# Sorting edges by destination before a graph layer: two buckets per scan, and sorted blocks added into DRAM tables by GpSimd

## The reference

```python
edge_index = jnp.stack([src, dst])                      # src is sorted differently from dst
# layer 0:  first row of edge_index is the target, second the source
w0f, w1f = x @ w0, x @ w1
x = layernorm(x + relu(w0f + segment_sum(w1f[edge_index[1]], edge_index[0], N)))
# layer 1: relational attention, 8 edge types, 8 heads of 32; softmax over each target's edges
x = layernorm(x + attention(x, W, attn_src, attn_dst, edge_index, edge_type))
```

## Time and profile before

| | us |
|---|---|
| median of 3 runs (2782.86 to 2790.21) | 2787.57 |
| span of the profiled execution | 2782.6 |
| DVE's first operation in the loop of moves | 134.99 |
| POOL's first gather of y | 288.67 |

### The profile page before, as it was taken

How to read it: one execution, slowest core, us unless ns; L and a number is a source line. 1 busy time by engine, 2 the same in 40 slices (tenths; PEclk the granted TensorE clock), 3 DMA queues, 4 the chain that set the end, 5 groups by cost and what they waited for, 6 DMA issues and landing times.

```text
span 2782.6 us, 38039 instructions
## 1 busy us (share of the span) xinstructions
PE 2296.5 (83%) x9879; PEld 1645.9 (59%) x9879; DVE 1984.8 (71%) x4237; ACT 1685.5 (61%) x3537; POOL 1843.1 (66%) x1874
## 2 busy tenths in 40 slices
PE   7866688899999999999988578777777777777775
PEld 4454566677777777777764456555555555555541
DVE  8999475555556555555553578888888888888887
ACT  4399455566666666566653466656656655665643
POOL 0000677777777777777771777777777777777745
PEclk9888799999999999999998688888888889888888
DMA  4300545764444444444454454545445545545535
GB/s 133 104 1 1 164 116 151 179 225 152 160 152 160 153 159 153 158 155 155 150 138 157 133 147 139 138 139 147 136 138 143 144 137 140 146 139 137 141 93 157
DMA packets 177746, 387.53 MB, mean 139 GB/s; under 512 B 42638, under 2 KB 106836, under 8 KB 171011
## 3 DMA queue, kind: packets, MB, share of 16 engines
q0 software_dynamic: 83888, 233.09, 30.6%
q1 hardware_dynamic: 86594, 99.05, 11.8%
q10 hardware_dynamic: 7056, 52.99, 4.9%
HBM read 302.96 MB, written 82.03 MB: 138 GB/s over the span
## 4 chain that ended last, share of the span: by engine, by line
PE 39%; POOL 24%; issue 12%; DVE 10%; DMA 9%; ACT 4%; DVEq 2%; SPq 0%; POOLq 0%; ACTq 0%; PEldq 0%
PE ps L1647 18%; POOL region L1287 15%; PE ps L1685 8%; POOL region L1245 7%; PE ps L1749 6%; DMA region<-ha_d,idx_t 5%; DVE nodes L839 4%; DMA region<-y_d,edge_z 3%; PE ps L1558 3%; ACT region L1374 2%; DVE nodes L721 1%; PE ps L1609 1%; PE ps L1732 1%; DVE region L444 1%; POOL region L1304 1%
## 5 line engine op out<-in xcount | busy, mean ns | idle before, releaser
L1245 POOL DMA_INDIRECT region<-y_d,edge_z x856 | 878.5, 1026 | 548.6 <-DVE edge_z L605 286.9
L1287 POOL DMA_INDIRECT region<-ha_d,idx_t x880 | 897.1, 1019 | 310.6 <-issue 240.8
L721 DVE TENSOR_TENSOR nodes<-ps,nodes 128x512 f32 x856 | 592.2, 692 | 491.4 <-PE ps L1647 377.7
L1647 PE MATMUL ps<-region 128*128 128x256 f32 x3424 | 794.3, 385 | 72.7 <-DMA region<-y_d,edge_z 26.3
L1647 PEld LDWEIGHTS ps<-region 128*128 128x128 f32 x3424 | 650.0, 192 | 249.2 <-issue 115.5
L1749 PE MATMUL ps<-region 128*128 128x264 f32 x1760 | 618.5, 482 | 163.5 <-DVE nodes L839 119.9
L1749 PEld LDWEIGHTS ps<-region 128*128 128x128 f32 x1760 | 347.5, 224 | 359.7 <-DVE nodes L839 237.1
L839 DVE TENSOR_TENSOR nodes<-ps,nodes 128x264 f32 x880 | 373.6, 425 | 52.1 <-DVE nodes L839 42.5
L1409 ACT ACTIVATE region<-iota_n,edge_z 128x256 f32<-128x256 f32 x856 | 364.7, 499 | 68.0 <-PE ps L1647 63.3
L1685 PE MATMUL ps<-region,edge_z 128*128 128x512 f32 x784 | 363.0, 592 | 3.3 <-ACT edge_z L1431 2.4
L1443 ACT COPY region<-ps 128x512 f32<-128x512 f32 x196 | 114.6, 587 | 350.7 <-PE ps L1685 289.6
(11 more groups left out here) (243 smaller groups left out, 1977.4 us busy)
## 6 DMA issues: line engine op xcount, KB each, us to landing
ha_d<-region ACTq DMA_DIRECT2D x49, 1056.0 KB, 4.7
region<-near_d SPq DMA_DIRECT2D x55, 512.0 KB, 5.0
region<-ha_d,idx_t POOLq DMA_INDIRECT x880, 3.3
region<-y_d,edge_z POOLq DMA_INDIRECT x856
edge_z<-level_d SPq DMA_DIRECT2D x55, 136.0 KB, 3.3
kl_d<-region SPq DMA_DIRECT2D x8, 903.0 KB, 15.5
edge_z<-kl_d SPq DMA_DIRECT2D x55, 129.0 KB
y_d<-edge_z SPq DMA_DIRECT2D x25, 256.0 KB, 3.2
```

The costliest lines, as they stand in the source:

```text
L721: v.tensor_tensor(into, ps[:, u, :], into, ALU.add).then_inc(added0, 1)
L1245: g.indirect_dma_start(rows0[c % RING][:, u, :], None, y_d, bass.IndirectOffsetOnAxis(ap=y_idx[:, k:k + 1], axis=0), bounds_check=node_bou ...
L1287: g.indirect_dma_start(rows[s][:, k, :], None, ha_rows, bass.IndirectOffsetOnAxis(ap=idx_t[:, B * b + k:B * b + k + 1], axis=0), bounds_ch ...
L1647: mm = t.matmul(ps[:, u, h * D:(h + 1) * D], lhsT=sel0[c % SEL][:, u, h * P:(h + 1) * P], rhs=rows0[c % RING][:, u, :], start=True, stop=True)
```

## The change

- Buckets are taken in pairs: 13 masks of the pair (9 on DVE, 4 on ACT) whose value is 1 for the even and 4096 for the odd bucket. So one count and one scan carry both; counts, starts and q are packed and unpacked by shifts and ands. The scans are 13.
- `wide` and its broadcast go. DVE and POOL make `jumps` over 104 windows x 25 buckets (2600 elements) between scans, DVE sums it to `goes_row`, and PE turns it behind y tile 20, for which PE waits.
- A window has 32 cells. A move still takes 28 columns of edges, but as two groups of 14, each with its own 104 windows in its own half of the bank; the matmuls are 28 of 104 by 64 columns. DVE sums high and low part into `stage` (four buffers).
- POOL adds each group's 104 rows of 32 cells into a table in DRAM by an indirect DMA that accumulates (60 in all). There are three tables in turn, and the n-th place waits until the (n-3)-th has landed. SP fills the tables with zeros early and reads them back at the end in two parts; DVE adds the three, PE turns them, ACT copies the cells out. `halves`, `S_c` and `settle` go.
- y tiles 36 to 49 are made in the loop, one behind each second move. In it ACT makes the Abs of its next window in four parts.

```diff
-    PP = 4
-    TB = PP * BLK
-    NBT = -(-(-(-E // KR)) // PP)
-    HC = P // 2
-    WW = (TB * P + BK * (2 * HC - 2)) // HC
+    PP = 2
+    TBG = PP * BLK
+    TB = 2 * TBG
+    NBT = -(-(-(-E // KR)) // (2 * PP))
+    NG2 = 2 * NBT
+    HC = P // 4
+    WW = (TBG * P + BK * (2 * HC - 2)) // HC
+    NPAIR = -(-BK // 2)
+    HIGH = 4096
+    NTAB = 3
     COLS = -(-((E + BK * (P - 1)) // P) // 8) * 8
     NG = COLS // 4
     RING = 5
     SEL = 3
-    OH = COLS // 2
-    MASKED = 18
-    EARLY = BK - MASKED
-    WIDE_AT, WAB_AT = 20, 28
+    OH = 4 * P
+    MASKED = 9
+    EARLY = 6
+    GOES_AT, WAB_AT, Q_AT = 20, 28, 35
+    WROWS = KR * P // HC
...
+    place_d = [dram(f"place{n}_d", [WROWS, HC], F32) for n in range(NTAB)]
...
+            do(v.tensor_scalar(bit_i, loc_i, 1, None, ALU.bitwise_and))
+            do(v.tensor_scalar(pair_i, src_i, 9, None, ALU.logical_shift_right))
+            do(v.tensor_scalar(shift_i, bit_i, 12.0, None, ALU.mult))
+            do(v.tensor_scalar(c_row, bit_i, float(HIGH - 1), 1.0, ALU.mult, ALU.add))
+            do(v.tensor_copy(pair, pair_i))
             for t in range(MASKED):
-                v.tensor_scalar(masks[t], bt, float(t), 0.0, ALU.is_equal, ALU.add,
-                                accum_out=cnt[:, t:t + 1]).then_inc(masked, 1)
+                v.scalar_tensor_tensor(out=masks[t], in0=pair, scalar=float(t), in1=c_row, op0=ALU.is_equal, op1=ALU.mult,
+                                       accum_out=cnt_all[:, t:t + 1]).then_inc(masked, 1)
+            v.wait_ge(masked, MASKED)
+            v.wait_ge(counted, NPAIR - MASKED)
+            do(v.tensor_copy(cnt_i[:, 0, :], cnt_all))
+            do(v.tensor_scalar(cnt_i[:, 1, :], cnt_i[:, 0, :], 12, None, ALU.logical_shift_right))
+            do(v.tensor_scalar(cnt_i[:, 0, :], cnt_i[:, 0, :], HIGH - 1, None, ALU.bitwise_and))
+            v.tensor_copy(cnt, cnt_i.rearrange("p b t -> p t b")).then_inc(counted, 1)
...
-            do(v.scalar_tensor_tensor(out=start, in0=base, scalar=float(-HC), in1=before_p, op0=ALU.mult, op1=ALU.add))
-            do(v.scalar_tensor_tensor(out=start, in0=start, scalar=-1.0, in1=col_128, op0=ALU.add, op1=ALU.add))
-            SU["wd"] = n[0]
-            v.wait_ge(masked, MASKED)
-            v.wait_ge(counted, BK - MASKED)
+            do(v.scalar_tensor_tensor(out=starts, in0=base, scalar=float(-HC), in1=before_p, op0=ALU.mult, op1=ALU.add))
+            do(v.tensor_tensor(starts, starts, col_128, ALU.add))
+            do(v.scalar_tensor_tensor(out=start_all, in0=start[:, :, 1], scalar=float(HIGH), in1=start[:, :, 0],
+                                      op0=ALU.mult, op1=ALU.add))
...
-            for t in range(BK):
+            for t in range(NPAIR):
                 if t == 1:
                     v.wait_ge(sort_in, IN["v"])
                 if t >= 2:
                     v.wait_ge(summed, t)
-                v.tensor_tensor_scan(ranks[t % 2], ones[:, 0:1].to_broadcast([P, KR]), masks[t], start[:, t:t + 1],
+                v.tensor_tensor_scan(ranks[t % 2], ones[:, 0:1].to_broadcast([P, KR]), masks[t], start_all[:, t:t + 1],
                                      ALU.mult, ALU.add).then_inc(scans, 1)
                 if t >= 1:
                     put(t - 1)
-            put(BK - 1)
-
-
-            v.wait_ge(sort_in, IN["wide"])
-            do(v.scalar_tensor_tensor(out=jumps, in0=wide[:, :, 0:BK], scalar=part[:, 0:1], in1=wide[:, :, BK:2 * BK],
-                                      op0=ALU.is_le, op1=ALU.mult))
-            do(v.tensor_reduce(goes_f, jumps, X, ALU.add))
-            do(v.tensor_scalar(goes_i, goes_f, part[:, 0:1], None, ALU.add))
-            do(v.tensor_scalar(col_i, goes_i, 1, None, ALU.logical_shift_right))
-            do(v.tensor_scalar(odd_i, goes_i, 1, None, ALU.bitwise_and))
-            do(v.tensor_copy(goes_col, col_i))
-            SU["goes"] = n[0]
-            do(v.tensor_copy(sides[:, 1, :], odd_i))
-            do(v.tensor_scalar(sides[:, 0, :], sides[:, 1, :], -1.0, 1.0, ALU.mult, ALU.add))
-            v.tensor_scalar(part_i, v_col, 11, 4, ALU.logical_shift_right, ALU.logical_shift_left).then_inc(split_made, 1)
-            v.tensor_scalar(v_col, v_col, 2047, None, ALU.bitwise_and).then_inc(split_made, 1)
-            v.wait_ge(split_made, 2)
-            v.tensor_copy(v_high, part_i).then_inc(split_made, 1)
-            v.tensor_scalar(v_low, v_col, 2.0 ** -7, None, ALU.mult).then_inc(split_made, 1)
+                if t == 1:
+                    v.tensor_tensor(jumps, iota_row[:, 0:WW].unsqueeze(2).to_broadcast([P, WW, BK]),
+                                    wd[:, 0, :].unsqueeze(1).to_broadcast([P, WW, BK]), ALU.is_ge).then_inc(goes_made, 1)
+                if t == NPAIR // 2:
+                    v.wait_ge(goes_made, 2)
+                    do(v.tensor_reduce(goes_row, jumps, X, ALU.add))
+                    v.tensor_tensor(goes_row, goes_row, iota_row[:, 0:WW], ALU.add).then_inc(goes_made, 1)
+                if t == NPAIR // 2 + 1:
+                    v.tensor_scalar(part_i, v_col, 11, 4, ALU.logical_shift_right, ALU.logical_shift_left).then_inc(split_made, 1)
+                    v.tensor_scalar(v_col, v_col, 2047, None, ALU.bitwise_and).then_inc(split_made, 1)
+                if t == NPAIR // 2 + 2:
+                    v.wait_ge(split_made, 2)
+                    v.tensor_copy(v_high, part_i).then_inc(split_made, 1)
+                    v.tensor_scalar(v_low, v_col, 2.0 ** -7, None, ALU.mult).then_inc(split_made, 1)
+            put(NPAIR - 1)
+            v.wait_ge(summed, NPAIR + 1)
+            do(v.tensor_copy(place_i, q_row))
+            do(v.tensor_tensor(place_i, place_i, shift_i, ALU.logical_shift_right))
+            do(v.tensor_scalar(place_i, place_i, HIGH - 1, None, ALU.bitwise_and))
+            v.tensor_copy(q_row, place_i).then_inc(summed, 1)
...
-            def halves_of(k):
+            def stage_of(k):
                 v.wait_ge(moved, k + 1)
-                if k >= 2:
-                    v.wait_ge(o_ps, k - 1)
-                v.tensor_tensor(halves[k % 2][0:WW, :, :, :],
-                                ps[0:WW, 2 + k % 2, 0:2 * HC].rearrange("p (v n) -> p v n", v=2).unsqueeze(2)
-                                .to_broadcast([WW, 2, 2, HC]),
-                                sides[0:WW, :, k].unsqueeze(1).unsqueeze(3).to_broadcast([WW, 2, 2, HC]),
-                                ALU.mult).then_inc(halves_made, 1)
+                if k >= 4:
+                    for n in range(2 * k - 8, 2 * k - 6):
+                        v.wait_ge(placed[n % NTAB], 16 * (n // NTAB + 1))
+                v.tensor_reduce(stage[k % 4][0:WW, :, :],
+                                ps[0:WW, 2 + k % 2, 0:4 * HC].rearrange("p (s v n) -> p s n v", s=2, v=2),
+                                X, ALU.add).then_inc(staged, 1)
...
+            sp.wait_ge(iotas, 3)
+            sp.wait_ge(w_in, 32)
+            for n in range(NTAB):
+                sp.dma_start(place_d[n].rearrange("(p w) e -> p (w e)", p=P), zeros).then_inc(w_in, 16)
...
+            for n in range(NTAB):
+                sp.wait_ge(placed[n], 16 * ((NG2 - n + NTAB - 1) // NTAB))
+            for h, (first, end) in enumerate(CELLS):
+                end = min(-(-end // P) * P, KR)
+                for n in range(NTAB):
+                    sp.dma_start(table[n][:, first:end].rearrange("c (b s) -> c b s", s=P),
+                                 place_d[n].rearrange("(b c w) e -> c b (w e)", c=P, w=P // HC)
+                                 [:, first // P:end // P, :]).then_inc(table_in[h], 16)
...
+            g.wait_ge(goes_made, 1)
+            g.tensor_tensor(jumps, jumps, wd[:, 1, :].unsqueeze(1).to_broadcast([P, WW, BK]), ALU.mult).then_inc(goes_made, 1)
+
+            def place(n):
+                if n == 0:
+                    g.wait_ge(sort_in, IN["goes"])
+                    g.wait_ge(w_in, 16 * (NTAB + 3))
+                if n % 2 == 0:
+                    g.wait_ge(staged, n // 2 + 1)
+                if n >= NTAB:
+                    g.wait_ge(placed[n % NTAB], 16 * (n // NTAB))
+                g.indirect_dma_start(place_d[n % NTAB], bass.IndirectOffsetOnAxis(ap=goes_i[0:WW, PP * n:PP * n + 1], axis=0),
+                                     stage[n // 2 % 4][0:WW, n % 2, :], None, bounds_check=place_bound, oob_is_err=True,
+                                     compute_op=ALU.add).then_inc(placed[n % NTAB], 16)
+
+            for n in range(NG2):
+                place(n)
...
+            windows_of(0, 0, TB)
             for k in range(NBT):
-                columns_of(k)
-                if k % 4 == 1 and k + 3 < NBT:
-                    windows_of(k + 3)
+                ahead = k // 4 * 4 + 4
+                if ahead < NBT:
+                    windows_of(ahead, TBG // 2 * (k % 4), TBG // 2 * (k % 4) + TBG // 2)
+                if y_tile_at(k) is not None:
+                    keep_products(y_tile_at(k))
...
```

(44 more changed lines are left out.)

184 lines of the change are left out of this document (97 added, 87 removed).

## The result

The changed kernel takes 2807.82 us (median of four runs, 2804.39 to 2812.3) against 2787.45 of the kernel before on the same chip: 1.0071 times as long, 95% interval 1.0055 to 1.0087. I had forecast 2740. The profiled execution after is the one of 2804.39 us, 1.8 more than its span. The span grew by 20.0 us. 18.0 of them lie ahead of the first gather of y, which starts at 306.70 and not at 288.67; behind it the work takes 2495.9 us, where it took 2493.9. So the question is the sort alone, 65.2 us from the forecast start (241.5) to the real one.

What follows compares the result with a forecast made beforehand. Before the loop PE's order was the bound; in it ACT and DVE were nearly full. First place at 126.4, 59 steps of 1.75 and a tail of 11.8 put the gather at 241.5, 47.2 sooner: 2787.6-47.2 = 2740.4 us, range 2722 to 2780.

Steps and rivals of the forecast that it cites:

- That is 1.72 a place: GpSimd's queue in the loop: each place takes 1.32 us of issue and gap plus 0.41 of hold.
- the queue is the bound by little: Loop of moves: GpSimd's queue at 1.75 us a place sets the pace, against 1.69 for the engines.
- Issue: GpSimd's queue: issuing one place costs 1.01 us, as a row gather does, and 0.30 until the next.
- Hold: GpSimd's queue: DVE operations with two SBUF inputs lengthen a place by 0.41 us on average.
- the landing: Loop: a place's round trip of 5.2 us, three in flight, allows one place per 1.75 us.
- the tail: From the last place's issue to the first gather of y: landing, loads, additions and shift take 11.8 us.
- The engines' own loop: Loop: a circle of move, Abs, kept tile and Relu takes 3.4 us a move; last move ends at 222.6.
- The gain ahead of the loop: Before the loop: fewer masks, scans and y tiles let PE turn q at 107, 22.5 us sooner.
- The first: Rival, loop: places hide wholly and the engines set the pace; gather at 236.4, -52.3 us, 2735; chance 0.26.
- The second: Rival, loop: a place's round trip is long, 6 to 7 us; -30 to -10 us, middle 2762; chance 0.20.
- third: Rival, loop: round trip from 7.5 us puts the gather behind 288.67; at 10 us +52, 2840; chance 0.10.
- DVE alone as the bound: Loop, variant of the rival with hidden places: DVE's 12.4 us for four moves set the pace; -58 us, 2729.

Runs made afterwards that it cites:

- e2: Changed kernel with the 60 places as plain indirect writes that replace rows, without the addition: 2772.58 us (one execution).
- e1: Changed kernel with DVE waiting in the loop for the end of each operation on two SBUF inputs before the next: 2760.56 us, 0.9913 of the kernel before.
- e4: Changed kernel with no places issued, only counted as landed, so y is gathered from row 0: 3189.94 us; moves 3.6 us each.
- e8: Changed kernel with both the DVE waits of e1 and the plain writes of e2: 3058.12 us, beside 3105.15 for the kernel before on that chip.
- e3: Changed kernel with two tables in DRAM instead of three: 2802.24 us (one execution).
- e7: Changed kernel with DVE's windows operation, from the fifth move, replaced by an equally long reduce with one SBUF input: 140.6 us from first to last place.
- e6: Changed kernel with one DVE wait a move, ahead of the windows: 0.9995 of the kernel before.

## Why the prediction was wrong

The step that failed is "That is 1.72 a place", and with it "the queue is the bound by little". The place was taken at 1.42 us of issue and hold, and took 2.46. Both terms were too small, and one for a reason that the rows could have given.

- Issue: I took 1.01 us from gathers, which add nothing. With the addition it is 1.60 (e2 against the changed kernel). 0.59 more a place, 35 us over 59 steps.
- Hold: I took +0.41 as a mean of three gathers beside fp32 operations. It was 2.46-1.60 = 0.86: 0.45 more, 27 us. The 0.41 was no property of the operations but of the gaps around them. Of the operations in the earlier trace rows the first ends at 488.50, and the others lie as far apart as in e1 (lines below). Each held gather there ends 0.89 behind the end of the one operation that it began under: 489.39 against 488.50, 492.83 against 491.94. In the loop up to four operations follow without a gap, 3.3 us in all, and the longest hold was 2.99 (4.59-1.60).

```profile
488.53 1.09 DVE L676 TENSOR_TENSOR region<-region 128x896 f32<-128x896 f32 x1
...
490.85 1.09 DVE L679 TENSOR_TENSOR region<-region 128x896 f32<-128x896 f32 x1
```

35 and 27 make the 62 us by which the first-to-last time of the places (165.2) passes its forecast (103.2); the 0.34 us between two places, for 0.30, is what I had added for the landing (1.75 for 1.72). The rest of the 65.2 is small: the first place 1.75 later (128.15, not 126.4), the tail 13.4 and not 11.8. The engines' own loop, 3.6 us a move and not 3.4 (e4), hides under the queue. The 27 us are the hold beyond what I had allowed for. The whole hold is 0.86 a place, 51 us, and e1 brings it down to 0.15 with nothing but gaps: 0.71 less a place, 42 us, which is what the places and the first gather gained (42.2 and 42.4). The division above is one of busy times, not of what each term would bring alone: without the addition (e2) the places gained 29.7 us, not 34.

What held: counts at 24.7 (26.1), scans from 39.4 (40.6), `goes_row` at 69.7 (68.0), q_row at 94.95 (93.7), q turned at 108.4 (107); in brackets the forecasts. The gain ahead of the loop is there: 21.1 us at the first move. The loop with its tail took 182.5 us from there (306.70-124.19), where it took 143.4: 39.1 were lost.

The rivals. The first (places hidden, 236.4) is not what this kernel does; e8 comes within 10.6 us of it. The second and third made the landing the bound. The outcome is on the third's side, past its turning point: it needed 2.5 us or more a place, and 2.80 came. But its mechanism is refuted: the landing is 3.2 us, less than the 5.2 I took, and with one table fewer the places took 3.9 us longer, not half as long again (e3). I had put the danger in the queue's length, rightly, and in the wrong member of it. My own mark, "wrong if the places come more than 2.4 us apart", was met. One more slip: the chance of slower, 0.10, hung on the landing alone, and the issue, of which the earlier trace rows showed disturbed cases, had no upper end of its own. The longest of the three, 1.82, with 0.30 would have made 2.12 a place, 263 for the gather, and the addition was in no row. In the first rival, DVE alone as the bound comes to -60 by the terms of the sum (7 times 1.1 less), not -58; nothing hangs on it.

The Trainium skill ("SBUF — State Buffer", "Who interferes with whom") says that a DVE instruction with two SBUF inputs shuts GpSimd out of its reads. The case agrees: 4.31 us beside four such operations, and e7, where a reduce with one input doesn't hold a place. Its inference that descriptor generation escapes a tensor_tensor doesn't hold for these indirect writes; 1.60 became up to 4.59. I had weighed that exception rightly and still given the hold a mean from rows with gaps.

**Shown:** the hold, by putting gaps (e1), by cutting the run (e6, e7); the price of the addition (e2, e8); that landings don't bound three tables (e3); the engines' own pace (e4). With the gaps the step of 2.08 us adds up: 1.60 undisturbed, 0.15 for the rest of the operation under which a place begins, 0.30 between two, and 3.0 us of waits over all 59 steps. **Open:** what an indirect DMA does in its first 0.12 us (1.60-1.48) that needs what DVE holds; why the second place got in between two operations of a run; and the 2.0 us more behind the first gather, which e1 (2493.7) does not have, and which are less than the spread of the executions (2804.39 to 2812.3).

## What to carry to other kernels

Before moving work to GpSimd's DMA queue, look at what DVE does at that time: operations with two SBUF inputs, back to back, shut it out to the end of the run, and a semaphore wait of DVE on its own last result lets it in. Here four such waits a move gave 42 us, and one gave 20 (e6). Take the price of an issue from the same kind of DMA (a gather isn't an adding write), and give an issue an upper end of its own, as much as a landing. When a queue of equal steps is the bound, an error of one microsecond in a step is multiplied by its count.

## What the runs showed of the hardware that I had not expected

The hold goes both ways. Beside GpSimd's 6.96 us multiplication, which ends at 54.21, one of DVE's scans took 5.82 us, where the next took 2.09; it ends 1.9 us behind the multiplication. No run tests this further.

```profile
50.28 5.82 DVE L545 TENSOR_TENSOR_SCAN ps<-ones,region 128x896 f32<-128x896 f32 x1
...
57.20 2.09 DVE L545 TENSOR_TENSOR_SCAN ps<-ones,region 128x896 f32<-128x896 f32 x1
```

These 3.7 us lie on DVE's way to `goes_row`, for which PE was waiting, and which came 1.7 us behind its forecast.

Gathers of one and the same row are slow. In e4, where all 856 gathers of y fetch row 0, they land after (us, shortest, median, longest):

```profile
DMA to landing us min/median/max: 3.7/13.6/30.3
```

In the changed kernel, with the rows that the sort gives, it is:

```profile
DMA to landing us min/median/max: 2.7/2.9/10.6
```

From the first gather to the end e4 took 2944 us, the changed kernel 2496; 433 of the 448 us lie between the first and the last of these gathers. A kernel whose indices are left at zero to measure something else pays for that.
